# When the input weights of eight experts are loaded and split: all raw weights in the place of their low parts, one split inside each early block

## The reference

```
x = x + 0.5 * ffn(layernorm(x))     # mixture of 8 experts, top 2 of 8
x = x + attention(layernorm(x))     # 16 heads, causal
x = x + 0.5 * ffn(layernorm(x))     # the same weights once more

ffn: logits = x @ router.T; the two best experts of a token, softmax of their two logits
     h = x @ w_in[e].T (1024 wide); a, b = halves of h
     out += gate * ((silu(a) * b) @ w_out[e].T)          for each token of expert e
```

## Time and profile before

| | us |
|---|---|
| timed runs, median of 3 | 452.99 |
| profiled execution, span | 448.6 |
| PE busy in the span | 401.3 (89%) |
| DVE busy | 302.4 (67%) |
| ACT busy | 257.7 (57%) |
| POOL busy | 269.0 (60%) |

### The profile page before, as it was taken

One profiled execution on the slowest core, in us unless ns is written; L12 is line 12 of the kernel. 1 busy time (PEld: TensorE's weight loads), 2 busy tenths in 40 slices (PEclk: granted clock), 3 DMA queues, 4 the chain that ended last, 5 costly groups with the idle time before them and its releaser, 6 DMA issues.

```text
span 448.6 us, 10288 instructions
## 1 busy us (share of the span) xinstructions
PE 401.3 (89%) x2892; PEld 330.1 (74%) x2893; DVE 302.4 (67%) x605; ACT 257.7 (57%) x630; POOL 269.0 (60%) x314
## 2 busy tenths in 40 slices
PE   7305999999999989889999999988899999999995
PEld 3302788888888876758788888766478888888884
DVE  6795855685565688697767677775556576655656
ACT  2561656555655645688778788832065565565552
POOL 5846874686547817857757777410255576755760
PEclk9555899999999999999999999998899999999999
DMA  8748841111212180000000000004571112211136
GB/s 276 287 187 300 282 136 58 47 57 37 70 49 49 43 273 8 1 1 3 4 0 0 0 0 0 1 1 153 162 249 53 54 35 70 59 58 47 47 85 222
DMA packets 25736, 38.87 MB, mean 87 GB/s; under 512 B 3056, under 2 KB 20720, under 8 KB 25712
## 3 DMA queue, kind: packets, MB, share of 16 engines
q1 hardware_dynamic: 19088, 24.41, 16.1%
q0 software_dynamic: 4544, 12.07, 8.9%
q10 hardware_dynamic: 2080, 2.10, 1.4%
HBM read 29.37 MB, written 9.19 MB: 86 GB/s over the span
## 4 chain that ended last, share of the span: by engine, by line
PE 65%; DVE 16%; DMA 7%; POOL 3%; ACT 3%; issue 3%; SPq 0%; DVEq 0%; ACTq 0%; POOLq 0%
PE bank L1326 24%; PE bank L1348 12%; PE bank L1483 7%; PE bank L1494 4%; PE bank L1336 4%; DMA arena<-xn_scratch,gather_row 3%; PE bank L1450 2%; PE bank L1302 2%; PE bank L1249 2%; DMA w_out<-y_scratch 2%; PE bank L1530 2%; DVE w_lo L892 2%; POOL w_lo L511 2%; DMA y_scratch<-arena,scatter_row 1%; PE bank L1484 1%
## 5 line engine op out<-in xcount | busy, mean ns | idle before, releaser
L524 POOL DMA_INDIRECT arena<-xn_scratch,gather_row x46 | 52.8, 1149 | 58.1 <-PE bank L1302 35.6
L530 POOL DMA_INDIRECT y_scratch<-arena,scatter_row x42 | 59.3, 1412 | 31.6 <-ACT arena L701 28.6
L1326 PE MATMUL bank<-w_hi,xT_hi 128*128 x184 | 62.4, 420 | 2.1 <-ACT xT_hi L664 2.1
L1018 DVE TENSOR_TENSOR wo_lo<-w_out,wo_hi 128x1024 fp32r<-128x1024 f32 x46 | 62.0, 1348 | 2.9 <-PE bank L1348 2.0
L1023 DVE TENSOR_TENSOR gT_lo<-bank,gT_hi 128x512 fp32r<-128x512 f32 x46 | 31.7, 690 | 45.4 <-ACT gT_hi L679 45.4
L1326 PE MATMUL bank<-w_lo,xT_hi 128*128 x184 | 58.0, 396 | 0.0
L1326 PE MATMUL bank<-w_hi,xT_lo 128*128 x184 | 57.8, 395 | 0.0
L617 POOL TENSOR_TENSOR k_head<-k_hi,head_mask 128x256 fp32r<-128x256 f32 x64 | 38.8, 627 | 28.8 <-PE bank L1484 21.7
L690 ACT ACTIVATE wo_hi<-w_out 128x1024 fp32r x46 | 48.8, 1061 | 9.5 <-issue 8.7
L672 ACT ACTIVATE arena<-bank 128x512 f32<-128x512 f32 x46 | 27.5, 598 | 42.9 <-PE bank L1326 42.9
L1007 DVE TENSOR_TENSOR xT_lo<-bank,xT_hi 128x256 fp32r<-128x256 f32 x46 | 19.5, 424 | 43.0 <-ACT xT_hi L664 43.0
(11 more groups left out here) (180 smaller groups left out, 979.9 us busy)
## 6 DMA issues: line engine op xcount, KB each, us to landing
w_out<-in_win_t SPq DMA_DIRECT2D x8, 1024.0 KB, 5.1
w_out<-in_wout_t SPq DMA_DIRECT2D x16, 512.0 KB, 6.0
w_out<-y_scratch SPq DMA_DIRECT2D x16, 256.0 KB, 4.4
xn_scratch<-arena ACTq DMA_DIRECT2D x2, 1024.0 KB, 6.1
x<-in_x SPq DMA_DIRECT2D x4, 256.0 KB, 3.7
out<-x SPq DMA_DIRECT2D x4, 256.0 KB, 2.2
arena<-xn_scratch,gather_row POOLq DMA_INDIRECT x46, 3.4
y_scratch<-arena,scatter_row POOLq DMA_INDIRECT x46, 3.0
```

What stands on the lines that cost most here:

```text
L524: pool.indirect_dma_start(out=xb[j % 2][:, :], out_offset=None, in_=xn_dram, in_offset=bass.IndirectOffsetOnAxis(ap=gather_row[:, j:j + 1] ...
L530: pool.indirect_dma_start(out=y_dram, in_=y[j % 2][:, :], in_offset=None, out_offset=bass.IndirectOffsetOnAxis(ap=scatter_row[:, j:j + 1], ...
L1018: dve.tensor_tensor(wo_lo[:, :, :], w_out[:, bass.ds(e, 1), :, :].rearrange("p o c d -> p (o c) d"), wo_hi[u][:, :, :].bitcast(F32), ALU.s ...
L1326: last = pe.matmul(bank[2 * half + u][:, :], tok[u][:, k, :], wts[:, bass.ds(e, 1), k, half * H:(half + 1) * H], start=(part == 0 and k == ...
```

## The change

1. **Place of the raw weights.** A new tile w_raw lies in the place of w_lo. SP loads each expert's raw weights into its own part of it, and the subtraction writes w_lo over w_raw. The three stages and SP's waits for a free stage are gone; so are the rooms in w_out.
2. **Order of the loads.** SP loads input weights 0 and 1, output weights 0, input weights 2; then it waits until the first two gathers have landed; then it issues output and input weights alternately (twelve loads), and the two bias rows. `pass_on_w_out` comes once, behind all of these.
3. **Place of the splits.** ACT's split is now two instructions of half an expert each. Experts 0 and 1 are split on ACT before `route` has its result, expert 2 before the first block. DVE keeps only the split of expert 0 ahead of `route`; those of experts 1 and 2 stand behind it. POOL splits expert 0, waits for `chosen_ready`, splits expert 1, and expert 2 between the second and the third gather. The splits of experts 3 to 7 stand in the steps j = 0 to 4 (expert j+3 in step j) on all three engines.
4. **At least one block for each expert** (`block_edge[:, 0:1]` is -1), so that block j never has an expert above j.
5. PEELED is 5 in place of 3 (for both ffn), and the matmuls without a use in the first ffn are 18, 6, 4 in place of 0, 8, 0, as they already were in the second one.

The core of the diff:

```diff
         w_hi = sb("w_hi", [P, E, DK, 2 * H], F32R)
+        with ExitStack() as room:
+            w_raw = room.enter_context(nc.sbuf_tensor("w_raw", [P, E, DK, 2 * H], F32))
         w_lo = sb("w_lo", [P, E, DK, 2 * H], F32R)
...
-WARM_START, WARM_RANKS, WARM_PLAN, WARM_TURNED = 12, (0, 18), (8, 6), (0, 4)
+WARM_START, WARM_RANKS, WARM_PLAN, WARM_TURNED = 12, (18, 18), (6, 6), (4, 4)
...
+            load_w_in(0)
+            load_w_in(1)
+            load_w_out(0)
+            load_w_in(2)
+            for parity in range(2):
+
+                sp.wait_ge(gathered[parity], 16)
+            for e in range(EARLY, E):
+                load_w_out(e - EARLY + 1)
+                load_w_in(e)
+            for e in range(E - EARLY + 1, E):
+                load_w_out(e)
...
-                    for e in range(TURN_AFTER):
-                        split_back(e)
+                    split_back(0)
+                    pool.wait_ge(chosen_ready, 1)
+                    split_back(1)
...
                 for j in range(SCATTERED):
+                    if f == 0 and j + EARLY < E:
+                        split_back(j + EARLY)
...
-                act.activation(w_hi[:, e, :, :], stage[e % STAGES][:, :, :], ACT.Copy).then_inc(w_hi_ready, 1)
+            def split_high(e, half):
+
+                act.wait_ge(win_loaded[e], 16)
+                act.activation(w_hi[:, e, half, :], w_raw[:, e, half, :], ACT.Copy).then_inc(w_hi_ready, 1)
...
                     copy_gT(f, j)
+                    splits = f == 0 and isinstance(j, int) and j + EARLY < E
+                    if splits:
+                        split_high(j + EARLY, 0)
                     if silu_next:
                         split_out(f, j + 1, 1 - u)
                     if copy_next:
                         copy_xT(f, j + 2, u)
+                    if splits:
+                        split_high(j + EARLY, 1)
...
                         split_out_low(f, j + 1, 1 - u, e)
+                    if f == 0 and isinstance(j, int) and j + EARLY < E:
+                        split_low(j + EARLY)
```

More of the change, by code:

```diff
@@ L253, in build @@
         attn_w_loaded = sem("attn_w_loaded")
-        stage_loaded = [sem(f"stage_loaded{i}") for i in range(STAGES)]
+        win_loaded = [sem(f"win_loaded{e}") for e in range(E)]
         w_hi_ready = sem("w_hi_ready")
@@ L398, in pass_on_w_out, with load_w_in @@
                     sp.sem_inc(wout_ready)
[L400 to L421, removed]
+            def load_w_in(e):
+                sp.dma_start(w_raw[:, e, :, :], win_in[e].rearrange("(k p) n -> p k n", p=P)).then_inc(win_loaded[e], 16)
+            load_w_in(0)
[9 more added lines that the diff above has]
+                load_w_out(e)
             for dst, src in ((bias_half, bias_in), (bo, bo_in)):
@@ L425, in _ @@
                 if f == 0:
-                    pass_on_w_out(0, range(free_experts, E))
+                    pass_on_w_out(0)
                 else:
@@ L488, in _ @@
             iota(block_edge[:, :], [[P, E]], 0, 0)
+            then(pool.memset(block_edge[:, 0:1], -1.0))
             then(pool.memset(expert_before[:, :, :], 1.0))
@@ L572, in ffn @@
                     if f == 0 and j == 2:
[L573 to L577, removed]
+                        split_back(2)
                     gather(f, j)
@@ L719, in ffn @@
                 if f == 0:
-                    for e in range(1, STAGES):
-                        split_front(e)
+                    for half in range(DK):
+                        split_high(0, half)
+                    for half in range(DK):
+                        split_high(1, half)
                 act.wait_ge(gap_ready, f + 1)
@@ L728, in ffn @@
                 if f == 0:
-                    for e in range(STAGES, TURN_AFTER + 1):
-                        split_front(e)
+                    for half in range(DK):
+                        split_high(2, half)
                 copy_xT(f, 0, 0)
-                if f == 0:
-                    for e in range(TURN_AFTER + 1, E):
-                        split_front(e)
                 silu(f, 0, 0)
@@ L985, in route @@
                 if f == 0:
-                    split_low(STAGES + 1)
+                    for e in range(1, EARLY):
+                        split_low(e)
                 dve.wait_ge(e1_ready, f + 1)
@@ L1086, in ffn @@
                 route(f)
-                if f == 0:
-                    split_low(TURN_AFTER)
                 copy_xT_low(f, 0, 0)
-                if f == 0:
-                    for e in range(TURN_AFTER + 1, E):
-                        split_low(e)
                 copy_xT_low(f, 1, 1)
```

28 lines of the change are left out of this document (7 added, 21 removed).

## The result

The changed kernel takes 462.19 us (median of four timed runs, 460.96 to 463.13), the kernel before 452.85 us beside it (four runs, 451.97 to 454.75). The ratio is 1.0218, 95% interval [1.0185, 1.0252]. The forecast was 447.2, range 441.5 to 453.5, so it was wrong in sign too. The profiled execution took 460.96 us with a span of 459.2: what lies around a span is 1.76 us. By that the profiled execution before took some 450.4, and 10.6 us of span have been added.

The account below looks back on a forecast made before the run. PE was taken to bound 65% of the span, with DVE, POOL and DMA holding the start. Block 3's turn at 47.9 plus 29.0 for five steps gave 76.9 for 82.71: 5.8 us won, 452.99 to 447.2, range 441.5 to 453.5.

Parts of the forecast that it names:

- Steps 1, 2: Logits to `chosen`, ending 18.3, before 21.55; then `chosen` to `gather_row`, ending 26.3, before 35.58, with a 0.85 us DVE wait.
- bound 0: Delay of the plan, ahead of `gather_row`, by the 18 warm matmuls: bounds 0 and 2 us, 0 taken.
- Step 3: First gather, up to the turn of block 0: 31.4, before 42.52; its issue beside two splits some 3.0 us.
- Step 4: Turn of block 0 to turn of block 2: 8.2 us by the second ffn's template, before 10.37.
- Step 5: New wait of ACT behind SP's 14 DMA issues, 7.1 us: cost 3.4 us, turn of block 3 at 47.9.
- rival C: SP's issues wait in a full queue, 1.28 us each, 14 taking 18: 10.8 us more, 458.0 us; chance 0.07.
- Step 6: Five loop steps with splits, DVE and POOL meeting at the port: 5.8 us each, 29.0 together, cost 4.4 us.
- Step 7: Everything after the five steps, including second ffn and attention: 0 change, bounds -0.5 and +0.5 us.
- A: The port doesn't bind in the steps, splits find gaps: 4.95 us a step, 443.0 us in all; chance 0.18.
- B: POOL's queue binds in the steps, gathers standing behind splits: 6.8 us a step, 452.2 us in all; chance 0.17.
- D: Early start isn't won, through PE's low clock or loads holding first steps: 2 to 5 us less, about 451; chance 0.08.

## Why the prediction was wrong, step by step

**Steps 1, 2: right, one term by luck.** 18.50 for 18.3 and 26.59 for 26.3. The wait of 0.85 in step 2 was put on a two-operand subtraction and came on a one-operand CAST (0.88 more than without a split). The 18 matmuls took 5.76, the 5.73 of the second ffn, and bound 0 was the right end of 0 to 2.

**Step 3: right, 0.5 us cautious.** Turn of block 0 at 30.90 for 31.4. The issue was 2.23 beside two splits, as it was beside one (2.24); I had said 3.0. The rule of the Trainium skill cited there (SBUF - State Buffer, "Who interferes with whom") would have DVE's two-operand subtraction leave descriptor making alone. The runs contradict it: 1.24 without a split beside it, 2.24 with, and 0.99 against 1.80 inside the steps; and PE's wait for the first gather, which doesn't rest on POOL's rough spans, fell by 1.0 us with it.

**Step 4: 1.9 us too little.** 10.11 from block 0 to block 2, not 8.2. The template from the second ffn has neither a split of POOL nor a train of this size there: SP issues four output weights from 323.58 on, when its gather 2 is already issued (322.98). 0.83 of the excess is a plain wait for gather 2, and 0.26 a wait for xT_lo, which stood on DVE behind `gate_p`, held up by POOL's split (below). The rest is in smaller pieces.

**Step 5: the step that failed.** It said that 14 issues take 14 x 0.51 = 7.1 us and ACT starts wo_hi at 40.0. They took 23.1, and ACT started at 55.56. From block 2 to block 3 went 24.04 in place of 8.3: 15.7 us, of which the low clock behind PE's 16 us of idleness is 2.7. The mechanism was there by name as rival C, with a chance of 0.07; but its price was wrong too (458.0, measured 462.19), since I took the longest issue seen, 1.28, as the cost of a full queue. In the kernel before the fullest moment that I find is 2,112 - 275 = 1,837 packets under way (at 326.4), about where blocking begins in the change, so no row of it bounds that cost; the bound had to be the DMA time of what is asked for. The twelve loads are 8.9 MB, 22 us at 404 GB/s. The last issue goes when some 2,000 packets are left, and the last loads are output weights in packets of 1 KB, so 2 MB are left and not 4: (8.9 - 2) / 404 GB/s is 17 us. The rest of the 23.1 is the slow start, beside gathers and scatters: 242 GB/s on average up to 41.42, where later it is 395. With early words block 3's turn comes 4.96 after block 2's. The Trainium skill ("Anatomy of one DMA" in DMA: Bandwidth & Descriptors) says of the path of GpSimd's DMAs that a lot of descriptors can be emitted before the added cost shows. SP's loads are in another queue (hardware_dynamic, where the gathers are software_dynamic), so the sentence did not bound them, and the prediction should not have leaned on it. For them the cost shows at about 2,000 packets, and issues of loads then take up to 6.78 us.

**Step 6: right.** 30.08 for 29.0, with the long DVE operations that it named and PE's waits for gT_lo (3.7 of 4.2 us idle). Long and short steps did not alternate as forecast: one of 5.25, then 6.31, 6.83, 5.68, 6.01. With POOL's split moved PE waits for DVE no more, and most steps are 5.28. (The prediction calls the last turn in this sum block 7's; 82.71 is that of block 8.)

**Step 7: not quite.** 2.0 us came back behind block 8, where I had 0 within 0.5.

The sum for block 8's turn is 18.2 us off: -0.5 + 1.9 + 15.7 + 1.1. **Rivals.** A: no, PE waits for DVE's subtractions. B: not in the change, whose steps have no wait for a gather; in the version with early words its waits do show. C: yes, at a higher price than its own. D: only the 0.83 for gather 2; the low clock of 2.7 us came later, from the pause.

## What to carry to other kernels

A semaphore signal must not stand behind DMA issues on the same queue: give it as soon as it is due, since an issue is cheap only while the queue has room (0.37 to 0.65 us here, then up to 4.05). Count the packets that a train of loads will have under way, and if it is more than the trace of before ever had, price the issue by the time that the DMA engines need for the surplus, not by the median issue. Start such a train when no small gather on the critical path is about to be issued, and have what the next steps need in memory ahead of it.

## What was not expected of the hardware

- SP's issues block by packets under way, at about 2,000 (1,700 to 2,300) in one queue, whether these are 2.0 MB or 4.2 MB; a blocked issue took up to 6.78 us.
- A software gather beside such a train landed 7.45 us after its issue; the page's median of the kernel before is 3.4.
- Some one-operand DVE instructions wait for POOL as well, others don't: in the change two TENSOR_REDUCE at 19.59 and 19.78, inside POOL's split of expert 1, took 0.28 and 0.21 as without it. But `gate_p`, 256 integers, took 2.81 us (0.23 in the second ffn) and ended as POOL's split, begun at 30.40, did (32.78):

```profile
30.00 2.81 DVE L981 TENSOR_SCALAR gate_p<-pair_i 128x2 int32<-128x2 int32 x1
```

```profile
30.40 2.38 POOL L501 TENSOR_TENSOR w_lo<-w_raw,w_hi 128x1024 fp32r<-128x1024 f32 x1
```
